# A decoder layer on one core: another hand-written order of the engines' steps in the fill, the repeats and the end

## What is computed

```python
x = x + self_attention(layernorm(x))                    # 16 heads of 16
x = x + cross_attention(layernorm(x), ctx, ctx, mask)   # 77 context tokens, int32 mask (0 -> -inf)
x = x + soft_moe(layernorm(x))

def soft_moe(x):                        # 8 experts x 128 slots
    xn, se = rms_norm(x, gamma_x), rms_norm(slot_embeds, gamma_slot)
    logits = xn @ se.T                                  # 256 x 1024
    slots = softmax(logits, over experts).T @ xn
    h = gelu(slots @ w1) @ w2                           # hidden 1024
    return softmax(logits, over all 1024 slots) @ h
```

## Time and profile before

| what | value |
|---|---|
| time, median of 3 runs (lowest, highest) | 1761.76 us (1760.68, 1763.05) |
| the profiled execution: time, span | 1763.35 us, 1761.6 us |
| TensorE, matmuls: busy | 1704.1 us, 97% of the span |
| DVE, ACT, POOL busy | 63%, 57%, 27% |
| granted clock of TensorE, mean | 0.994 |
| one batch of the repeated part | 103.35 us |

### The profile page before, as it was taken

How to read it: one execution, slowest core, us unless ns; L and a number is a source line. 1 busy time by engine, 2 the same in 40 slices (tenths; PEclk the granted TensorE clock), 3 DMA queues, 4 the chain that set the end, 5 groups by cost and what they waited for, 6 DMA issues and landing times.

```text
span 1761.6 us, 38281 instructions
## 1 busy us (share of the span) xinstructions
PE 1704.1 (97%) x15966; PEld 1531.3 (87%) x15966; DVE 1117.5 (63%) x2408; ACT 1009.9 (57%) x1713; POOL 471.9 (27%) x386
## 2 busy tenths in 40 slices
...
DMA packets 20842, 19.51 MB, mean 11 GB/s; under 512 B 9920, under 2 KB 19776, under 8 KB 20288
## 3 DMA queue, kind: packets, MB, share of 16 engines
...
...
## 4 chain that ended last, share of the span: by engine, by line
PE 85%; DVE 7%; issue 3%; ACT 3%; DMA 1%; SPq 1%; POOL 1%; POOLq 0%; DVEq 0%; ACTq 0%
PE ps L460 21%; PE ps L461 19%; PE ps L462 19%; PE ps L581 3%; PE ps L568 2%; PE ps L548 2%; PE ps L763 2%; PE ps L688 2%; PE ps L676 2%; PE ps L831 2%; PE ps L611 1%; PE ps L754 1%; PE ps L502 1%; ACT L1018 1%; DVE h_hi L1319 1%
## 5 line engine op out<-in xcount | busy, mean ns | idle before, releaser
L1448 POOL TENSOR_TENSOR h_lo<-h_f,h_hi 128x512 fp32r<-128x512 f32 x256 | 341.6, 1342 | 1006.9 <-DVE h_hi L1319 1006.9
L460 PE MATMUL ps<-sl_hi,w_hi 128*128 128x256 f32 x1024 | 303.1, 296 | 6.3 <-DVE sl_lo L1072 2.9
L460 PE MATMUL ps<-w_hi,h_hi 128*128 128x256 f32 x1024 | 300.8, 294 | 4.6 <-POOL h_lo L1448 3.7
L462 PE MATMUL ps<-w_lo,h_hi 128*128 128x256 f32 x1024 | 290.1, 283 | 0.0
L461 PE MATMUL ps<-w_hi,h_lo 128*128 128x256 f32 x1024 | 290.0, 283 | 0.0
L461 PE MATMUL ps<-sl_hi,w_lo 128*128 128x256 f32 x1024 | 289.2, 282 | 0.0
L462 PE MATMUL ps<-sl_lo,w_hi 128*128 128x256 f32 x1024 | 289.0, 282 | 0.0
L460 PEld LDWEIGHTS ps<-sl_hi,w_hi 128*128 128x128 f32 x1024 | 195.1, 191 | 30.4 <-ACT h_f L1018 18.4
L1319 DVE CAST h_hi<-h_f 128x512 fp32r<-128x512 f32 x256 | 119.1, 467 | 154.4 <-ACT h_f L1018 149.7
L460 PEld LDWEIGHTS ps<-w_hi,h_hi 128*128 128x128 f32 x1024 | 196.4, 192 | 11.2 <-POOL h_lo L1448 6.0
L461 PEld LDWEIGHTS ps<-w_hi,h_lo 128*128 128x128 f32 x1024 | 196.6, 192 | 0.0
...
## 6 DMA issues: line engine op xcount, KB each, us to landing
...
```

The source lines that it names most:

```text
L460: te.matmul(o, lhs[0], rhs[0], start=first, stop=False)
L462: return te.matmul(o, lhs[0], rhs[1], start=False, stop=last)
L1448: Q_.tensor_tensor(h_lo[:, part, :], h_f[:, part, :], h_hi[:, part, :].bitcast(f32), ALU.subtract)\
```

## The change

All operations on real data are the same, with the same operands; the tables put them in another order on PE, DVE, ACT and POOL. The identity products go from 167 to 161: 4 more ahead of `c0.k`, 2 each ahead of `d0.logits.0` and `m0.lt.0`, 6 behind `m0.dispatch.0`, 3 ahead of `c1.ob.1`, 1 ahead of `c1.scores.0`; 1 fewer each ahead of `c0.shifted.1` and `c0.mt.3`, 2 fewer ahead of `d0.q2`, none instead of 11 between `c1.v` and `d0.tr2.0`, 3 instead of 12 ahead of `m0.dispatch.0`. Some rows of the tables, and of the 13 repeats the two that the prediction comes to:

```diff
 ORDER = dict(
     pe="""
-        m.lt.0 l.outer.3.0 d.kv m.dispatch.0 l.outer.3.1 c.xt.1 m.slots.0 l.comb.3 d.xt.2 c.k c.q d.q2 m.hidden.0.0
+        m.lt.0 l.outer.3.0 d.kv m.dispatch.0 l.outer.3.1 c.xt.1 l.comb.3 m.slots.0 d.xt.2 c.k c.q d.q2 c.v
...
-        m.hidden.3.0 c.shifted.3 d.xt.3 m.combine.2 m.hidden.3.1 c.pv.3 m.hidden.3.2 c.tr.1 m.hidden.3.3 c.ob.1
-        d.logits.0 d.logits.1 d.logits.2 d.logits.3 c.oproj
+        c.mt.3 m.hidden.3.0 c.shifted.3 d.xt.3 m.combine.2 m.hidden.3.1 d.logits.0 c.pv.3 m.hidden.3.2 m.hidden.3.3
+        c.tr.1 d.logits.1 d.logits.2 c.ob.1 d.logits.3 c.oproj
...
 START = dict(
     pe="""
-        s0.idle.10 s0.idle.2 c0.xt.1 s0.idle.6 c0.k c0.q c0.v s0.idle.18 s0.idle.3 c0.scores.0 s0.idle.8 s0.idle.3
+        s0.idle.10 s0.idle.2 c0.xt.1 s0.idle.8 s0.idle.2 c0.k c0.q c0.v s0.idle.18 s0.idle.3 c0.scores.0 s0.idle.8
...
-        d0.q2 s0.se_transp.1.1 c1.xt.1 d0.scores2.0 c1.k c1.q d0.mt2.0 c1.v d0.shifted2.0 s1.idle.6 d0.scores2.1
-        d0.pv2.0 s1.idle.2 d0.mt2.1 s1.idle.3 d0.shifted2.1 d0.tr2.0 s1.idle.4 s1.idle.1 d0.ob2.0 c1.scores.0 d0.pv2.1
+        d0.q2 s0.se_transp.1.1 c1.xt.1 d0.scores2.0 c1.k d0.mt2.0 c1.q d0.shifted2.0 c1.v d0.scores2.1 d0.pv2.0
+        d0.mt2.1 d0.shifted2.1 d0.tr2.0 s1.idle.3 d0.ob2.0 s1.idle.3 c1.scores.0 d0.pv2.1 s1.idle.2 d0.tr2.1 s1.idle.4
...
-        d0.logits.1 d0.logits.2 d0.logits.3 m0.lt.0 s1.idle.3 s1.idle.3 s1.idle.3 s1.idle.3 m0.dispatch.0 c1.scores.2
-        c1.pv.1 m0.slots.0 c1.mt.2 c1.shifted.2 c1.tr.0 m0.hidden.0.0 c1.ob.0 c1.scores.3 c1.pv.2 m0.hidden.0.1
+        s1.idle.1 s1.idle.1 m0.lt.0 c1.scores.2 c1.pv.1 s1.idle.3 m0.dispatch.0 s1.idle.6 c1.mt.2 m0.slots.0
...
-        m0.hidden.2.2 d1.shifted2.0 m0.combine.1 d1.scores2.1 d1.pv2.0 m0.lt.3 d1.mt2.1 d1.shifted2.1 d1.tr2.0
-        c2.scores.1 m0.hidden.2.3 c2.mt.1 c2.shifted.1 d1.pv2.1 m0.dispatch.3 d1.ob2.0 c2.scores.2 c2.pv.1 d1.tr2.1
+        d1.scores2.1 d1.pv2.0 m0.hidden.2.2 d1.mt2.1 d1.shifted2.1 d1.tr2.0 m0.combine.1 m0.lt.3 c2.scores.1 d1.pv2.1
+        m0.hidden.2.3 c2.mt.1 m0.dispatch.3 d1.ob2.0 c2.shifted.1 d1.tr2.1 m0.outer.2.0 c2.scores.2 c2.pv.1 m0.slots.3
...
     dve="""
-        c0.stats.1 s0.lo.0 c0.xh.1 c0.xt.1 s0.columns s0.lo.1 c0.kd d0.mask c0.qd c0.v c0.kl c0.qs c0.mx.0 s0.gammas
+        c0.stats.1 c0.xh.1 s0.lo.0 c0.xt.1 s0.columns s0.lo.1 c0.kd c0.qd c0.v c0.kl c0.qs c0.mx.0 c0.sh.0 c0.mx.1
...
 FINISH = dict(
     pe="""
-        m-2.outer.1.1 d-1.mt2.1 m-2.slots.2 m-2.comb.1 d-1.shifted2.1 d-1.tr2.0 m-2.hidden.2.0 d-1.ob2.0
-        m-2.hidden.2.1 d-1.pv2.1 m-2.hidden.2.2 d-1.tr2.1 m-2.hidden.2.3 m-2.lt.3 d-1.ob2.1 m-2.combine.1 d-1.oproj2
+        m-2.outer.1.1 m-2.slots.2 d-1.mt2.1 m-2.comb.1 d-1.shifted2.1 d-1.tr2.0 m-2.hidden.2.0 d-1.ob2.0
+        m-2.hidden.2.1 m-2.hidden.2.2 d-1.pv2.1 m-2.hidden.2.3 d-1.tr2.1 m-2.lt.3 d-1.ob2.1 m-2.combine.1 d-1.oproj2
...
     dve="""
-        m-1.hid.0.2 l-2.finish m-1.hid.0.3 m-1.sl.1 m-1.cm.2 m-1.keep m-1.edn.2 m-1.row_max m-1.hid.1.0 m-1.cb.0
+        m-1.hid.0.2 m-1.hid.0.3 m-1.sl.1 m-1.cm.2 m-1.edn.2 l-2.finish m-1.row_max m-1.hid.1.0 m-1.cb.0 m-1.pr.0
```

More of the change, by code:

```diff
@@ new lines @@
+        m.hidden.0.0 m.hidden.0.1 m.hidden.0.2 d.scores2.0 m.hidden.0.3 m.lt.1 d.mt2.0 l.combine.3 d.shifted2.0
+        m.outer.0.0 c.scores.0 m.dispatch.1 m.outer.0.1 c.mt.0 m.slots.1 m.comb.0 c.shifted.0 d.pv2.0 m.hidden.1.0
+        m.hidden.1.1 d.scores2.1 c.pv.0 m.hidden.1.2 d.mt2.1 m.hidden.1.3 m.lt.2 m.combine.0 d.shifted2.1 d.tr2.0
+        m.outer.1.0 m.dispatch.2 d.pv2.1 c.scores.1 m.slots.2 m.comb.1 m.outer.1.1 c.mt.1 m.hidden.2.0 d.ob2.0
+        c.shifted.1 d.tr2.1 m.hidden.2.1 c.scores.2 c.pv.1 m.hidden.2.2 d.ob2.1 m.hidden.2.3 m.lt.3 c.mt.2 m.combine.1
@@ L58 @@
+        c.shifted.2 d.oproj2 m.dispatch.3 m.outer.2.0 c.tr.0 m.slots.3 c.ob.0 c.scores.3 c.pv.2 m.comb.2 m.outer.2.1
+        c.mt.3 m.hidden.3.0 c.shifted.3 d.xt.3 m.combine.2 m.hidden.3.1 d.logits.0 c.pv.3 m.hidden.3.2 m.hidden.3.3
+        c.tr.1 d.logits.1 d.logits.2 c.ob.1 d.logits.3 c.oproj
     """,
     act="""
-        m.ed.0 m.ds.0 c.xt.1 m.sl.0 l.pr.3 l.cb.3 d.xt.2 c.k c.q d.q2 m.ge.0.0 c.qh m.ge.0.1 m.ge.0.2 c.kh m.ge.0.3
-        m.ed.1 d.ex2.0 m.ds.1 m.ec.0 m.sl.1 m.cb.0 c.ex.0 d.xo2.0 m.ec.1 m.ge.1.0 m.ge.1.1 m.pr.0 m.ge.1.2 c.xo.0
@@ L69 @@
[L69 to L72, removed]
+        m.cm.0 d.mask d.stats.2 m.edn.0 c.stats.1 d.kv d.xh.2 c.xh.1 m.ds.0 c.xt.1 m.row_max m.sl.0 d.xt.2 l.cb.3
@@ new lines @@
+        c1.shifted.3 d1.kv m0.hidden.0.3 c1.pv.3 m0.lt.1 c1.tr.1 s1.idle.3 c1.ob.1 c1.oproj m0.outer.0.0 m0.dispatch.1
+        m0.outer.0.1 c2.xt.1 m0.slots.1 m0.comb.0 c2.k c2.q m0.hidden.1.0 m0.hidden.1.1 c2.v d1.xt.2 m0.hidden.1.2
+        m0.hidden.1.3 m0.combine.0 m0.lt.2 c2.scores.0 d1.q2 m0.outer.1.0 m0.dispatch.2 c2.mt.0 c2.shifted.0
+        m0.slots.2 m0.comb.1 d1.scores2.0 m0.outer.1.1 d1.mt2.0 m0.hidden.2.0 d1.shifted2.0 c2.pv.0 m0.hidden.2.1
+        d1.scores2.1 d1.pv2.0 m0.hidden.2.2 d1.mt2.1 d1.shifted2.1 d1.tr2.0 m0.combine.1 m0.lt.3 c2.scores.1 d1.pv2.1
@@ L102 @@
+        m0.hidden.2.3 c2.mt.1 m0.dispatch.3 d1.ob2.0 c2.shifted.1 d1.tr2.1 m0.outer.2.0 c2.scores.2 c2.pv.1 m0.slots.3
+        c2.mt.2 m0.comb.2 c2.shifted.2 d1.ob2.1 m0.outer.2.1 c2.tr.0 c2.scores.3 m0.hidden.3.0 d1.oproj2 m0.hidden.3.1
+        c2.mt.3 c2.pv.2 c2.shifted.3 m0.hidden.3.2 d1.xt.3 m0.hidden.3.3 c2.pv.3 d1.logits.0 d1.logits.1 c2.ob.0
+        m0.combine.2 c2.tr.1 d1.logits.2 c2.ob.1 d1.logits.3 c2.oproj
     """,
     act="""
-        s0.hi.0 s0.hi.1 c0.xt.1 c0.k c0.q c0.kh c0.qh s0.hi.2 s0.se_squares c0.ex.0 c0.xo.0 c0.ex.1 c0.xo.1
@@ L105 @@
[L105 to L108, removed]
+        s0.hi.0 s0.hi.1 c0.xt.1 c0.k c0.q c0.kh c0.qh s0.hi.2 s0.se_squares c0.ex.0 c0.xo.0 c0.ex.1 s0.se_hi.0.0
```

105 lines of the change are left out of this document (55 added, 50 removed).

## The result

The changed kernel takes 1751.24 us (median of 4 runs, 1748.72 to 1752.68) against 1762.4 us, 0.9936 of the time before with a 95% interval of 0.9919 to 0.9953. That is 11 us faster, half of the 21.3 us that were forecast, and 2.2 us above the range. The profiled execution took 1750.94 us, its span is 1749.1.

The account below looks back on a forecast made before the run. TensorE, 1704.1 us busy in a 1761.6 us span, was the bound, leaving at most 57.5 idle plus low-clock loss. Terms -11.3, -1.4, -0.8, -7.3, -1.0 and +0.5 sum to -21.3, giving median 1740.5 us; range 1733 to 1749.

Parts of the forecast that it names:

- 5, the repeats: The 13 repeated batches: only neighbours swap, one or two switches between kinds go per batch; -1.0 us.
- The fill to the first quad: Start of kernel: moved mask step -8.4, earlier k -1.2, no low clock window -1.7; sum -11.3 us.
- The rest of the fill: From 79 to 247 us: shorter TensorE waits and a low clock window gone; -1.4, -0.8 and -7.3 us.
- The long low window near 207: Half-clock window beginning at 206.96 us, behind waits of 190 to 214; its going was put at -4.3 us.
- The first term: First cross-attention and c1, 79 to 97 us: ex2.0 starts earlier, c1.scores.0 at 95.4 instead of 96.77; -1.4 us.
- rival A: The clock falls once more, in 84 to 100 or near 207 us; costs 4.3, giving 1745 us; chance 0.2.
- The second term: Start of m0, 121 to 131 us: real steps replace identity products in the wait for the dispatch softmax; -0.8 us.
- rival D: Slower: ob.1 waits on nrm.1 in each of thirteen batches; 1765 us; chance 0.05.
- 6, the end: End of kernel: dispatch.0 moves earlier, finish later, slots.2 and hidden.2.2 change place; balance +0.5 us, between -1 and +2.
- The 1.0 for finish: At the end, finish behind sl.1 and edn.2 on DVE removes about half of hidden.1.0's 1.9 us wait; -1.0 us.
- the 0.6 given back: At the end, row maxima behind the moved finish come later and give back some 0.6 us.
- the 1.2 for mt2.1 and ob2.0: At the end, moving slots.2 and hidden.2.2 ahead leaves little cover before mt2.1/shifted2.1 and ob2.1; +1.2 us.

Follow-up runs that it names:

- mask_only: The kernel before with one DVE step moved, d0.mask from before c0.qd to behind c0.sh.3; 1754.19 us, ratio 0.9954.
- start_only: The kernel before with only the new table for the fill, repeats and end as before; 1745.07 us, ratio 0.9899.
- repeats_only: The kernel before with only the new table for the repeats, fill and end as before; 1766.00 us, ratio 1.0019.
- start_tail: start_only with the new order in only the tail of each repeat (from hidden.3.1 on TensorE); 1750.19 us, ratio 0.993.
- start_head: start_only with the new order of the repeats except their tail, which stays as before; 1754.46 us, ratio 0.9952.
- head_xt3: start_head with one ACT swap in the repeats taken back, c.ex.3 ahead of d.xt.3 again; 1747.21 us, ratio 0.9906.
- start_products: start_only with 10 more identity products in the fill, at five places between 60 and 90 us; 1744.47 us, ratio 0.9899.

## Why the prediction was wrong

The forecast was -21.3, the profiled execution gained 12.4, the medians 11.2. The step that failed is 5, the repeats. By the prediction's own steps:

1. **The fill to the first quad, -11.3: right**, by its size (-11.35 at `shifted.1`) and by its mechanism (mask_only: -8.47 and -1.7). Inside, two errors cancel, and that is luck: k came at 11.16, 0.7 better than I had it (with equal tables it comes from 10.76 to 12.15), and the cast beside POOL's add, which I had not seen, took 0.8 away.
2. **2 to 4. The rest of the fill, -9.5 (1.4 + 0.8 + 7.3)**: from `shifted.1` to `c2.oproj` it is -6.4 in after and -8.5 in start_only. The long low window near 207 went, as forecast, and from `m0.hidden.0.0` to `c2.oproj` 7.0 of 7.3 came, 3.2 of it idle time (forecast 3.0). The first term was right in start_only, -1.25 for -1.4; in after it is +1.0, because the clock fell twice for 3.4 us, at 64.8 and 81.8. That is rival A, in a place (84 to 100) near the one named and in another that I hadn't looked at. It had 0.2; five of the eight profiles with this START have such a window, so it is the usual case, not the odd one. Its price is smaller than the 4.3 I gave it: from `scores.0` to `c1.scores.0` it is 63.0 us in the three profiles without a window, 1.2 to 1.4 more in the three with 3.4 us of low clock and 2.0 to 2.3 more in the two with 6.8. The second term gave -0.45 for -0.8 in both.
3. **5, the repeats, -1.0: the failed step.** It reads "only neighbours swap" and "by my count one or two such switches go per batch: -0.08". Measured is +0.19 per batch, +2.9 in the profile (2.5 from the 0.19, the rest from two longer batches) and +3.3 (1.6 to 5.1, from the ratio) alone in repeats_only. The term had the wrong sign and was 3.9 us off. The price of a switch, 0.05 to 0.1, was near; the count was wrong. It was of the swaps, not of all entries into a run: logits split in three enter twice more, at about 0.1 each. start_tail shows it, +0.22 with the new tail alone. And I looked for waits at the steps that moved, and found their slack good (nrm.1 and ob.1: no wait, rival D did not come). A wait that I didn't look for lies two engines away: ACT's swap of xt.3 and ex.3 makes ge.3.0 late by 0.56 (start_head, head_xt3). In after it costs nothing only because the split logits hide it.
4. **6, the end, +0.5: near, but for the clock.** +2.4 in the profile, of which 1.5 is the window at 1733.9, which start_tail has too with FINISH of before. Without it +0.9, all of it waits (10.3 instead of 9.5 us in sum). The 1.0 for finish was right (0.91), the 0.6 given back is 0.2, and the 1.2 for mt2.1 and ob2.0 is 1.4. The wait of 2.0 us at dispatch.0 was missed, but waits of 0.88 and 0.98 went for it.

The errors are 3.9 (repeats), 3.0 (fill, 1.8 of them the two windows, as start_only shows) and 1.9 (end, 1.5 of them a window), together the 8.9 us between -21.3 and -12.4. All three point the same way, and the range had taken them one at a time: A's 4.3 leads to 1745, and only with the repeats at their bound as well, 4.9 above their term, is it 1749.7. Without its three windows the profiled execution would have taken about 1747.6 us, inside the range, and of its four runs the one with the highest mean clock, 0.999, took 1748.72. That the median came out above the range took both the repeats and the clock.

The Trainium skill, TensorE: Matmul & The Clock Gate, part "A second HAM failure mode: psum-queue depth-cycling", weighed in the prediction, puts a falling clock down to frequent short idles between groups of matmuls. The two windows in the fill of after agree: no gap above 1.06 us stands within 20 us ahead of them. start_only, with the same gaps and no window, shows that such gaps don't bring a window each time; that products in them stop it isn't shown (start_products).

What stays open: why one execution of a kernel has a window and the next has not. That a short window comes in one execution and not in another with the same table of START is shown; what decides isn't.
